# Making the node table first and gathering 32 chunks of source rows into an on-chip ring beside the count of destinations, in a four-layer graph network on one core

## What is computed

```
def _gat_layer(x, src, dst, W, a_s, a_d, b, heads, outc):
    h = (x @ W).reshape(N, heads, outc)
    alpha_s = (h * a_s).sum(-1)
    alpha_d = (h * a_d).sum(-1)
    e = jax.nn.leaky_relu(alpha_s[src] + alpha_d[dst], SLOPE)
    m = jax.ops.segment_max(e, dst, num_segments=N)
    p = jnp.exp(e - m[dst])
    z = jax.ops.segment_sum(p, dst, num_segments=N)
    alpha = p / (z[dst] + 1e-16)
    out = jax.ops.segment_sum(h[src] * alpha[:, :, None], dst, num_segments=N)
    return out.reshape(N, heads * outc) + b
```

## Time and profile before

| | us |
|---|---|
| median of 3 timed runs | 27099.24 (27094.47 to 27100.72) |
| profiled execution, its own time | 27162.9 |
| span of the profiled execution | 27161.2 |
| steps 1 and 2 (up to 862) | 862 |
| step 3 (862 to 1057) | 194 |
| steps 4 and 5 (1057 to 1240) | 183 |
| step 6, gat1 (1240 to 5209) | 3969 |
| everything behind it | 21952 |

### The profile page before, as it was taken

The page is one execution under the profiler, slowest core; times in us unless marked ns, Lnnn a source line. Parts: engine busy times, 40 slices in busy tenths (PEclk is TensorE's granted clock), DMA queues, the critical chain, the costliest instruction groups (busy, mean ns, idle before and its releaser), DMA issues. The chain is left out here.

```text
span 27161.2 us, 315919 instructions
## 1 busy us (share of the span) xinstructions
PE 16179.7 (60%) x98805; PEld 12079.2 (44%) x98808; DVE 16979.6 (63%) x40579; ACT 3692.9 (14%) x7407; POOL 19454.9 (72%) x17570
## 2 busy tenths in 40 slices
PE   4200000046666656888854888888888367777773
PEld 3200000035555534666633444444444256666662
DVE  9466666437777734666652666666666457676764
ACT  0000000022222221111101111111111011111110
POOL 0477777667777746777753777777777678888885
PEclk6555555555555556888865888888888678888886
DMA  3111111111111100111120111111111200000002
GB/s 123 46 32 33 32 33 32 26 18 32 31 31 32 31 16 20 24 25 24 25 71 10 20 19 19 19 20 19 19 19 19 68 19 20 21 20 21 20 21 69
DMA packets 1032557, 815.73 MB, mean 30 GB/s; under 512 B 602134, under 2 KB 922910, under 8 KB 1028512
## 3 DMA queue, kind: packets, MB, share of 16 engines
q0 software_dynamic: 561792, 189.30, 5.6%
q1 hardware_dynamic: 366264, 291.81, 4.1%
q10 hardware_dynamic: 104400, 333.49, 3.1%
HBM read 416.39 MB, written 396.80 MB: 30 GB/s over the span
## 5 line engine op out<-in xcount | busy, mean ns | idle before, releaser
L1352 POOL DMA_INDIRECT msgs<-msg_msg,msg_pos x4875 | 6814.5, 1398 | 1566.6 <-issue 1449.1
L873 POOL DMA_INDIRECT gat_got<-table,gat_idx x6250 | 5967.9, 955 | 1909.1 <-issue 1904.8
L1562 POOL DMA_INDIRECT sheaf_got<-table,sheaf_idx x3125 | 3245.9, 1039 | 953.3 <-issue 952.5
L1262 PE MATMUL sheaf_dps<-sheaf_dhotq,sheaf_dleft 128*128 128x392 bf16 x18000 | 3312.7, 342 | 0.7 <-DVE sheaf_dhotq L1247 0.7
L1262 PE MATMUL msg_dps<-msg_dhotq,msg_dleft 128*128 128x392 bf16 x16500 | 3282.7, 354 | 0.0
L1380 DVE TENSOR_TENSOR_SCAN msg_own<-keep_d,msg_own,msg_ex 128x25 f32<-128x25 f32 x6000 | 1091.0, 258 | 2412.1 <-DMA msg_ex<-ex 2412.1
L1403 PE MATMUL msg_fps<-ident,msg_outer 128*128 128x128 f32 x9375 | 1699.7, 332 | 1471.7 <-DVE msg_outer L1389 1471.7
L335 PE MATMUL hist_s_counts<-hist_s_hot_k,hist_s_hot_a 128*98 128x128 bf16 x3125 | 362.8, 313 | 3575.1 <-DVE hist_s_hot_k L288 3575.1
L1176 PE MATMUL place_look_ps<-place_nexts,place_hot_at 98*128 98x128 f32 x5000 | 1629.6, 466 | 1336.1 <-DVE place_same L1084 921.7
L1262 PEld LDWEIGHTS sheaf_dps<-sheaf_dhotq,sheaf_dleft 128*128 128x128 bf16 x18000 | 1818.5, 102 | 1262.0 <-issue 179.4
L1262 PEld LDWEIGHTS msg_dps<-msg_dhotq,msg_dleft 128*128 128x128 bf16 x16500 | 1740.6, 111 | 1136.3 <-issue 316.2
(11 more groups left out here) (465 smaller groups left out, 27670.1 us busy)
## 6 DMA issues: line engine op xcount, KB each, us to landing
gat_got<-table,gat_idx POOLq DMA_INDIRECT x6250
msg_ex<-ex SPq DMA_DIRECT2D x250, 400.0 KB
gat_sums<-gat_acc ACTq DMA_DIRECT2D x125, 675.0 KB, 3.3
msgs<-msg_msg,msg_pos POOLq DMA_INDIRECT x4875
tail_m<-msgs SPq DMA_DIRECT2D x75, 800.0 KB, 6.3
src_sums<-tail_acc ACTq DMA_DIRECT2D x75, 800.0 KB
gat_sums<-gat_acc ACTq DMA_DIRECT2D x125, 425.0 KB, 2.7
ex<-zeros ACTq DMA_DIRECT2D x25, 2000.0 KB
```

The lines of the kernel that those rows point to most:

```text
L873: pool.indirect_dma_start(got[b][:, j, :], None, table, bass.IndirectOffsetOnAxis(idx[b][:, j:j + 1], 0)).then_inc(gathered[b], 16)
L1262: last = pe.matmul(self.acc[:, n, 0:self.BQ], left[:, s_, t, :], hot_q[:, t, n * self.BQ:(n + 1) * self.BQ], start=False, stop=False, skip ...
L1352: pool.indirect_dma_start(msgs, bass.IndirectOffsetOnAxis(pos[b][:, j:j + 1], 0), msg[b][:, j, :], None).then_inc(scattered[b], 16)
L1562: pool.indirect_dma_start(got[b][:, j, :], None, table3, bass.IndirectOffsetOnAxis(idx[b][:, j:j + 1], 0)).then_inc(gathered[b], 16)
```

## The change

The weights, the node rows and `node_product("att1")` come first, without the writes to `ex4`. Then `count_destinations` runs with a stream for POOL of its own: 800 indirect DMAs that fetch the source rows of chunks 0 to 31 into `ring`, which has 32 places of one chunk in SBUF. All source numbers lie in SBUF as `src_all`, loaded once. Then come `find_segments("d")`, and a block `put1` in which POOL writes `alpha_d` to `ex4`. In gat1 POOL gathers only chunks 32 to 124, written out without a loop; chunk i goes into place i % 32 once DVE has finished chunk i - 32. DVE reads its rows from the ring, and waits for no gather in the first 32 chunks. The second attention (gat2) keeps the old way.

```diff
@@ count_destinations
-        def count_destinations(zeros):
+        def count_destinations(zeros, table, src_all, ring):
...
+                @block.gpsimd
+                def _(pool):
+                    for i in range(AHEAD):
+                        for j in range(CW):
+                            c = i * CW + j
+                            pool.indirect_dma_start(ring[:, i, j, :], None, table,
+                                                    bass.IndirectOffsetOnAxis(src_all[:, c:c + 1], 0)).then_inc(ahead_got, 16)
+                    pool.wait_ge(ahead_got, 16 * CW * AHEAD)
@@ attention, SP
-                        if not first:
-                            sp.wait_ge(gathered[b], 16 * CW * turn)
-                        sp.dma_start(idx[b][:, :], src_v[:, bass.ds(i * CW, CW)]).then_inc(idx_in[b], 16)
+                        if ring is None:
+                            if not first:
+                                sp.wait_ge(gathered[b], 16 * CW * turn)
+                            sp.dma_start(idx[b][:, :], src_v[:, bass.ds(i * CW, CW)]).then_inc(idx_in[b], 16)
@@ attention, POOL
-                    run_turns(pool, NCH, body)
+
+                    def follow(i):
+                        pool.wait_ge(done, i - AHEAD + 1)
+                        if i >= AHEAD + 2:
+                            pool.wait_ge(gathered[i % 2], 16 * CW * (i // 2 - AHEAD // 2))
+                        pool.sem_inc(admitted, 1)
+                        for j in range(CW):
+                            c = i * CW + j
+                            pool.indirect_dma_start(ring[:, i % AHEAD, j, :], None, table,
+                                                    bass.IndirectOffsetOnAxis(src_all[:, c:c + 1], 0)
+                                                    ).then_inc(gathered[i % 2], 16)
+                    if ring is None:
+                        run_turns(pool, NCH, body)
+                    else:
+                        for i in range(AHEAD, NCH):
+                            follow(i)
@@ attention, DVE
-                        dve.wait_ge(gathered[b], 16 * CW * (turn + 1))
-                        g_a = got[b][:, :, feats:feats + heads].rearrange("p t f -> p f t")
+                        if ring is None:
+                            dve.wait_ge(gathered[b], 16 * CW * (turn + 1))
+                        elif not stashed:
+                            dve.wait_ge(gathered[b], 16 * CW * (turn + 1 - AHEAD // 2))
+                        g_a = rows(i, b)[:, :, feats:feats + heads].rearrange("p t f -> p f t")
@@ the program
-            count_destinations(zeros)
-
-        with ExitStack() as ctx:
             fresh = sb("fresh", [P, C], F32, ctx)
-            find_segments("d")
...
+                ring = sb("ring", [P, AHEAD, CW, 20], F32, c2)
+                src_all = sb("src_all", [P, C], I32, c2)
...
-                load_all("weights1", [(w1_sb[:, :], L0_gnn_W1), (w2_ext[:, 0:C2], L0_gnn_W2),
+                load_all("weights1", [(src_all[:, :], src_v), (w1_sb[:, :], L0_gnn_W1), (w2_ext[:, 0:C2], L0_gnn_W2),
...
-                             put=(e1r, ex4), store=(t1r, table1))
-            renew_semaphores()
-            attention("gat1", H1, D, table1, 20, gat1_sums, last1, CountSources())
+                             store=(t1r, table1))
+                renew_semaphores()
+                count_destinations(zeros, table1, src_all, ring)
+                find_segments("d")
+                put_rows("put1", None, None, e1r, ex4, 4)
+                c3.close()
+                renew_semaphores()
+                attention("gat1", H1, D, table1, 20, gat1_sums, last1, CountSources(), src_all, ring)
```

More of the change, by code:

```diff
@@ L10 @@
 LANES = 4
+AHEAD = 32
 ALU = mybir.AluOpType
@@ L816, in _, with attention @@
                     pool.wait_ge(put, 16)
-        def attention(name, heads, feats, table, tw, sums, last_rows, extra):
+        def attention(name, heads, feats, table, tw, sums, last_rows, extra, src_all=None, ring=None):
             w = heads * (feats + 1)
@@ L826, in attention @@
             with ExitStack() as ctx:
-                idx = [sb(f"{name}_idx{b}", [P, CW], I32, ctx) for b in range(2)]
-                got = [sb(f"{name}_got{b}", [P, CW, tw], F32, ctx) for b in range(2)]
+                if ring is None:
+                    idx = [sb(f"{name}_idx{b}", [P, CW], I32, ctx) for b in range(2)]
+                    got = [sb(f"{name}_got{b}", [P, CW, tw], F32, ctx) for b in range(2)]
                 ex = [sb(f"{name}_ex{b}", [P, CW, 4], F32, ctx) for b in range(2)]
@@ L888, in _, with rows, ask @@
                     ch = Chain(dve, steps)
-                    def ask(i, b, turn, first):
+                    def rows(i, b):
+                        if ring is None:
+                            return got[b][:, :, :]
+                        return ring[:, bass.ds(i % AHEAD, 1), :, :].rearrange("p o t w -> p (o t) w")
+                    def ask(i, b, turn, first, stashed=False):
                         ch.begin(i)
@@ L916, in weigh @@
                     def weigh(i, b, turn, first):
-                        g_x = got[b][:, :, 0:feats].rearrange("p t f -> p f t")
+                        g_x = rows(i, b)[:, :, 0:feats].rearrange("p t f -> p f t")
                         dve.wait_ge(said, i + 1)
@@ L935, in weigh, with turn_of @@
                         dve.wait_ge(done, i + 1)
-                    run_turns_woven(dve, NCH, lambda now, before: extra.vector(dve, now, before, ask, weigh))
+                    def turn_of(i, b, turn, first, stashed):
+                        extra.count(dve, i, b, turn, first)
+                        ask(i, b, turn, first, stashed)
+                        weigh(i, b, turn, first)
+                    if ring is None:
+                        run_turns_woven(dve, NCH, lambda now, before: extra.vector(dve, now, before, ask, weigh))
+                    else:
+                        turn_of(0, 0, 0, True, True)
+                        turn_of(1, 1, 0, True, True)
+                        with dve.Fori(1, AHEAD // 2) as k:
+                            turn_of(2 * k, 0, k, False, True)
+                            turn_of(2 * k + 1, 1, k, False, True)
+                        with dve.Fori(AHEAD // 2, NCH // 2) as k:
+                            turn_of(2 * k, 0, k, False, False)
+                            turn_of(2 * k + 1, 1, k, False, False)
+                        turn_of(NCH - 1, 0, NCH // 2, False, False)
                     dve.tensor_copy(last_rows[:, :], acc[0][:, CW - 1, :])
@@ L977, in vector_start, with count @@
                 self.hist.dve_start(dve)
[L979 to L983, removed]
+            def count(self, dve, i, b, turn, first):
+                self.hist.dve(dve, i, b, turn, first)
             def vector_end(self, dve):
@@ L1825, in gnn_kernel @@
             w2_ext = sb("w2_ext", [HC1, C2 + 2], F32, ctx)
-            t2 = sb("t2", [NP, NK, 36], F32, ctx)
             with ExitStack() as c2:
[L1828 to L1831, removed]
+                ring = sb("ring", [P, AHEAD, CW, 20], F32, c2)
+                src_all = sb("src_all", [P, C], I32, c2)
+                c3 = c2.enter_context(ExitStack())
+                zeros = sb("zeros", [P, CW * EXW * 5], F32, c3)
+                setup(zeros)
+                w1_sb, a1 = sb("w1_sb", [D, HC1], F32, c3), sb("a1", [D, 2, HC1], F32, c3)
+                a2 = sb("a2", [HC1, 2, C2], F32, c3)
+                att_w, prod1, prod2 = sb("att_w", [D, 2, H1], F32, c3), sb("prod1", [D, 2, HC1], F32, c3), sb(
+                    "prod2", [HC1, 2, C2], F32, c3)
                 on_vector("clear_w1", lambda dve, ch: ch.add(dve.memset(w1_blocks[:, :], 0.0)))
-                load_all("weights1", [(w1_sb[:, :], L0_gnn_W1), (w2_ext[:, 0:C2], L0_gnn_W2),
+                load_all("weights1", [(src_all[:, :], src_v), (w1_sb[:, :], L0_gnn_W1), (w2_ext[:, 0:C2], L0_gnn_W2),
                                       (a1[:, 0, :], spread(L0_gnn_a_src1.rearrange("h c -> (h c)"), D, HC1)),
@@ L1839, in gnn_kernel @@
                          + [(w1_blocks[h * D:(h + 1) * D, h * C1:(h + 1) * C1], L0_gnn_W1[:, h * C1:(h + 1) * C1])
-                            for h in range(H1)], c2)
+                            for h in range(H1)], c3)
                 def weights(dve, ch):
@@ L1851, in gnn_kernel @@
                 on_vector("weights1_made", weights)
-                t1r, e1r = sb("t1r", [NP, NK, 20], F32, c2), sb("e1r", [NP, NK, 4], F32, c2)
+                t1r, e1r = sb("t1r", [NP, NK, 20], F32, c3), sb("e1r", [NP, NK, 4], F32, c3)
                 def rows1(dve, ch):
@@ L1865, in gnn_kernel @@
                 node_product("att1", [D], whole_groups(x_cur), [att_w[:, :, :].rearrange("p s h -> p (s h)")], 2 * H1, use1,
[L1866 to L1868 removed]
+                             store=(t1r, table1))
[6 more added lines that the diff above has]
```

(2 more changed lines are left out.)

4 lines of the change are left out of this document (1 added, 3 removed).

## The result

The changed kernel takes **26431.06 us** (median of 4 runs, 26422.13 to 26434.87) against 27099.98 us of the kernel before on the same chip (4 runs, 27094.47 to 27113.98): ratio 0.9752, 95% interval 0.9735 to 0.9769. The forecast was 26404 us. The profiled execution took 26433.71 us, its span is 26432.0 us.

What follows compares the result with a forecast made beforehand. POOL's number of gathers was taken to bound gat1, and DVE the count. Terms 127 + 1006 + 194 + 167 + 2980 = 4474 us against 5169, 695 less, gave 26404 us; range 26345 to 26520.

Steps and rivals of the forecast that it cites:

- Start stretch: Before the count: node product, table store, `src_all` load and leaving the block take 127 us, with no clock gain.
- the other bound: Node product in the start stretch: if TensorE's 71 us were halved by a faster clock, 36 us would go.
- The count: Count block with 800 gathers beside it: POOL becomes the bound at 1006 us, DVE's part being 823 us.
- Segments: Stage after the count: unchanged at 194 us.
- writes to `ex4` with gat1's start: After the segments: the writes alone take 167 us, and gat1's start 4.2 us.
- gat1: First attention's gathers: 21.6 us to POOL's start, 93 chunks in 2936 us on POOL, 18 us to DVE's end.
- DVE meets POOL at chunk 92: In gat1: DVE uses up the 32 chunks' lead by chunk 92, then waits for 33 chunks, about 345 us.
- The sum: From the count's old start to gat1's DVE end: 4474 us against 5169, 695 us less.
- Held-off gathers: Count: one-hots let one gather through per chunk, block 1787 us, kernel 27185 us; sign turns at 2.12 us a gather; chance 0.02.
- The zero fill in the way: Count: POOL waits behind the fill's DMA packets, likely +60 to +180 us, kernel 26460 to 26590 us; chance 0.10.
- DVE becomes gat1's bound: gat1: DVE needs over 23.8 us a chunk; at 24.5 it is 88 us more, kernel 26490 us; chance 0.03.
- The long unrolled stream: POOL's 3,125 straight-code gathers: fetching at 0.05 us each would add 156 us, kernel 26560 us; chance 0.03.

Runs made afterwards that it cites:

- experiment 2: Changed kernel's order only (table first, `ex4` written by itself), no gathers in the count, no ring, gat1 as before: 27285.21 us, ratio 1.0044 to the kernel before.
- experiment 7: Changed kernel, with POOL in the count waiting for its gathers of two chunks back, on two semaphores in turn: 26464.12 us, ratio 0.9743 to the kernel before.
- experiment 8: Changed kernel, with the count's comparison numbers in SBUF instead of PSUM, so both one-hot inputs lie in SBUF: 26978.69 us, ratio 0.9932 to the kernel before.
- experiments 4 and 5: Changed kernel with 26 chunks ahead instead of 32: the first with 26 ring places, 26466.94 us; the second with 32 places, 26429.57 us.

## Why the prediction was right, step by step

The measured 26431 us is 27 us above the forecast and inside its range (26345 to 26520), and the path is the foreseen one: POOL bounds the count and gat1, and DVE waits late in gat1 only. Part of the closeness is luck, since the largest errors have opposite signs.

- **Start stretch: 127 us forecast, 124.0 measured** (39.86 to 163.88). From the store's issue to the count's first operation are 6.2 us. The load of `src_all` costs 2.6 us, the difference to experiment 2 without it (163.88 against 161.25); the forecast had 3. The product gained nothing, as forecast: PE was busy 71.19 us for its 384 matmuls, 71.20 before, and from the first staged group to the last row written it took 104.3 us, against 105.3. But the reading behind that term was wrong, and that it held is luck. The prediction took from the earlier trace rows that matmuls cost the same at a granted clock of 1.00 and of 0.50. The trace has no record of the clock before 77.3 us in the kernel before, nor before 229.4 us in the changed kernel, and a window without a record prints 1.00. Three windows of the count before (PE busy and its matmuls, clock, DMA share, GB/s) tell more, the first inside a stretch recorded at 1.00 (from 169.5 us), the second ahead of all records, the third at 0.50:

```profile
172.46:172.86 0.40, 0.40 (x7) 1.00 0.00 0
61.40:61.80 0.40, 0.40 (x4) 1.00 1.05 432
100.60:101.00 0.40, 0.40 (x4) 0.50 0.00 0
```

  The same matmuls come at 56 ns in the first and at 107 ns in the other two. So the earlier trace rows compare one level with itself, and the product ran at the level of 0.50 in both kernels, as its equal busy time says. How much of the other bound's 36 us full clock would have saved, no run shows.
- **The count: 1006 forecast, 1027.2 measured.** This is the term that was mis-sized. POOL bounds it as foreseen, DVE's last operation ends after 827.8 us (forecast 823; 3.3 us of it are waits for its loads of `hist_d_key`), and a gather costs 1.25 us. Missing were the seven pauses, 25 us in all. The earlier trace rows held one, 3.14 us before the 128th mark; it was read as part of the marks' block and not carried over to a stream of 800; the prediction even says that the marks show 0.30 us between them. Leaving took 2.7 us instead of the 4 taken, and the 800 gathers without their pauses 998.5 instead of 1002.
- **Segments 194 and 194.1; writes to `ex4` with gat1's start 167 + 4.2 and 171.6.** As forecast.
- **gat1: 2976 us from DVE's start by the forecast's terms, and 1.9 to `zero_s`; 2968.0 measured.** POOL's first gather comes after 22.4 us (forecast 21.6). Its 2,324 spacings average 1.2587 us ((4504.4 - 1579.2)/2324), 31.47 us a chunk, so 93 chunks take 2927 us and not 2936. The forecast took 1.263 from the kernel before. The difference lies in the gathers' own mean, 954 ns (2217.92/2325) against 958 (2994.13/3125 of the earlier trace rows). Three of the four ns are the step from 947 to 944 in the median that experiment 7 tells of; its cause is open, so this part of the gain is not explained.
- **DVE meets POOL at chunk 92, 33 waits, 345 us: measured chunk 96, 29 waits, 289 us.** DVE needs 21.4 us a chunk ((3598.74 - 1564.95)/95), not 21.1. With that and 31.47 the forecast's own equation gives 94.7. It changes nothing in the time, since POOL sets the end.
- **The sum:** -3.0 for the start, +21.2 for the count, +0.5 for segments and writes, -9.9 for gat1 make the 9 us between 695 and 686. The other 18 of the 27 us are the net of two larger ones outside it. The part behind gat1 took 43 us less in the profiled execution after (21907 against 21950), which the forecast had left as it was. And the forecast took 64 us off for the distance of a profiled execution from its median, which was 63 us before and only 3 after, so 61 too much.

**The rivals.** *Held-off gathers*: not here, as the 944 ns show, but experiment 8 made it happen. Two gathers slipped in per chunk (255 in 827 us), where the rival supposed one, so a gather cost 1524/800 = 1.9 us, under its deciding point of 2.12, and even then the kernel stayed 0.7% ahead of before. *The zero fill in the way*: no. The DMA share in the count rose to 0.35, and the median gather did not move (944 ns). *DVE becomes gat1's bound*: no, 29 waits are left. *The long unrolled stream*: no; its 0.05 us were assumed, and no run shows them. 2,325 gathers in straight code show 0.305 us between them (707.9/2323), like the loop before, and none has a pause. Two things that the prediction priced without making them rivals: the ring holds POOL up once, as forecast, and the order does cost 108 us; experiment 2 is the kernel in which it decides.

**What stays open.** The pauses come after every 113 gathers of 128 rows and go when POOL waits for landings of its own; an increment alone does not remove them. That wait is never seen to hold POOL up (longest gap 0.3 us). Why 113, and whether the wait or the second semaphore does it, was not told apart; nor why the 128 marks, of 98 partitions each, have one such pause before the last. The block's end is short (2.7 us) where a pause lay 9 gathers back (the changed kernel and experiment 8), and long where it lay 85 back (8.9 and 9.0 in experiments 4 and 5) or there was none (10.2). That fits one piece of work on the queue that is done either in a pause or at the end, but this is argued only.

## What to carry to other kernels

When an engine bounds a loop by the number of its instructions, look for a stretch in which it is idle and its inputs can be made ready early; the gain ends where the added work outlasts what covers it (26 and 32 chunks gave the same time), and the costs of the new order are paid from the first chunk on. Give a ring more places than the lead that is filled ahead, so that the producer doesn't begin the next stage by waiting. Before gathers are put beside DVE's large operations, see that one of their inputs lies in PSUM; here that decided 497 us (gat1's end at 5023.3 in experiment 8, against 4526.6).

## What the runs showed of the hardware

- In the count, a run of indirect DMAs on POOL that never waits for its own landings stands still for 3.2 to 6.3 us after each 113 of them (128 rows each). With a wait for those of two chunks before, the 800 have none longer than 0.3 us, but the block then needs 10.2 us to end instead of 2.7, unless other work covers it.
- A `tensor_tensor` of DVE with both inputs in SBUF holds an indirect DMA on POOL (0.94 us) for 2.8 to 3.1 us and is itself not slowed (3484 against 3480 ns); with one input in PSUM neither is slowed (median gather 944 ns, DVE's operation 3480 ns).
- TensorE's matmuls of the histogram follow each other at 56 ns where a granted clock of 1.00 (2.4 GHz) is recorded, and at 107 ns at 0.50 (1.2 GHz). A window ahead of the first record of the clock prints 1.00 as well, though the matmuls come at 107 ns there: look at the spacing before reading such a 1.00 as full clock.
